# Mixture-of-experts tail of a graph and attention layer: expert rows scattered to token order inside the loop and reloaded densely

## What is computed

```
logits = xt @ router_w.T + router_b;  probs = softmax(logits)
topk_p, topk_i = top_k(probs, 2)
gates = sum(one_hot(topk_i) * topk_p)
for each expert e:
    h = gelu(xt @ w1[e].T + b1[e])
    acc += (h @ w2[e].T + b2[e]) * gates[:, e]
x = x + acc
```

## Time and profile before

| | us |
|---|---|
| median of 3 runs (lowest to highest) | 781.33 (780.14 to 784.73) |
| the profiled execution, its own time | 778.04 |
| its span, first to last record | 776.3 |
| PE busy | 699.3 (90%) |
| DVE busy | 456.4 (59%) |
| ACT busy | 232.4 (30%) |
| POOL busy | 132.5 (17%) |

### The profile page before, as it was taken

One profiled execution on the slowest core, in us unless ns is written; L12 is line 12 of the kernel. 1 busy time (PEld: TensorE's weight loads), 2 busy tenths in 40 slices (PEclk: granted clock), 3 DMA queues, 4 the chain that ended last, 5 costly groups with the idle time before them and its releaser, 6 DMA issues.

```text
span 776.3 us, 12270 instructions
## 1 busy us (share of the span) xinstructions
PE 699.3 (90%) x3759; PEld 450.8 (58%) x3760; DVE 456.4 (59%) x1388; ACT 232.4 (30%) x472; POOL 132.5 (17%) x191
## 2 busy tenths in 40 slices
PE   4888899999999999999999999999995499999934
PEld 2544455455555555555555788989783366676610
DVE  5538754278778787787854984353555233323336
ACT  2312211223233233232333333333342143344300
POOL 6055431000000000000000900020211110000064
PEclk9999999999999999999999999999996599999955
DMA  9600000073452707172555900010238695333467
GB/s 293 186 0 1 1 0 2 0 273 121 166 190 97 287 2 271 54 286 86 203 204 174 391 2 0 1 56 28 82 121 340 236 370 187 133 122 110 133 193 231
DMA packets 48883, 109.30 MB, mean 141 GB/s; under 512 B 6842, under 2 KB 6858, under 8 KB 46384
## 3 DMA queue, kind: packets, MB, share of 16 engines
q1 hardware_dynamic: 43616, 85.82, 30.7%
q0 software_dynamic: 4912, 20.60, 7.8%
q10 hardware_dynamic: 288, 2.10, 0.7%
HBM read 47.35 MB, written 61.16 MB: 140 GB/s over the span
## 4 chain that ended last, share of the span: by engine, by line
PE 79%; issue 5%; DVE 5%; POOL 4%; DMA 3%; ACT 2%; SPq 1%; POOLq 0%; DVEq 0%; ACTq 0%
PE bank L1284 12%; PE bank L1267 10%; PE bank L1435 7%; PE bank L1166 7%; PE bank L1235 7%; PE bank L1203 7%; PE bank L1448 6%; PE bank L1379 6%; PE bank L1322 6%; PE bank L1246 4%; PE bank L1307 4%; POOL arena L624 2%; PE bank L1406 2%; DMA arena<-in_wqkv 2%; DVE arena L887 1%
## 5 line engine op out<-in xcount | busy, mean ns | idle before, releaser
L887 DVE TENSOR_SCALAR arena<-iota,arena 125x128 f16<-125x128 f16 x392 | 113.2, 289 | 43.3 <-PE bank L1166 31.9
L889 DVE TENSOR_SCALAR arena<-iota,arena 125x320 f16<-125x320 f16 x392 | 120.3, 307 | 0.0
L698 ACT ACTIVATE arena<-bank 128x416 f32<-128x416 f32 (+1 forms) x120 | 62.3, 519 | 154.8 <-PE bank L1267 151.8
L1284 PE MATMUL bank<-arena 128*64 128x416 f32 (+1 forms) x480 | 97.2, 525 | 0.9 <-DVE arena L928 0.9
L928 DVE TENSOR_SCALAR arena<-bank 128x416 f32<-128x416 f32 (+1 forms) x120 | 68.1, 589 | 49.2 <-PE bank L1267 49.0
L1166 PE MATMUL bank<-arena 125*128 125x320 f16 x392 | 72.0, 302 | 8.7 <-DVE arena L889 8.5
L1235 PE MATMUL bank<-arena 128*128 128x416 f32 (+1 forms) x192 | 74.5, 537 | 2.7 <-DMA arena<-in_wqkv 1.4
L1435 PEld LDWEIGHTS bank<-arena 128*128 128x128 f32 x448 | 53.0, 198 | 20.7 <-issue 20.7
L1106 DVE COPY arena<-arena 128x1024 f32 x30 | 20.8, 694 | 74.5 <-issue 63.7
L1435 PE MATMUL bank<-arena 128*128 128x128 f32 x448 | 55.3, 283 | 9.9 <-issue 9.9
L1166 PEld LDWEIGHTS bank<-arena 125*128 125x128 f16 x392 | 32.4, 98 | 46.6 <-DVE arena L889 20.3
(11 more groups left out here) (228 smaller groups left out, 1171.4 us busy)
## 6 DMA issues: line engine op xcount, KB each, us to landing
slots<-arena SPq DMA_DIRECT2D x6, 5376.0 KB, 17.1
slots<-arena SPq DMA_DIRECT2D x2, 5120.0 KB, 16.5
arena<-in_ew POOLq DMA_DIRECT2D x9, 1024.0 KB, 7.0
arena<-slots SPq DMA_DIRECT2D x32, 256.0 KB, 2.8
slots<-arena SPq DMA_DIRECT2D x28, 256.0 KB, 2.0
arena<-in_ew SPq DMA_DIRECT2D x5, 1024.0 KB, 10.7
arena<-in_x SPq DMA_DIRECT2D x8, 512.0 KB, 6.9
arena<-in_gw SPq DMA_DIRECT2D x2, 2048.0 KB, 17.5
```

The costliest lines, as they stand in the source:

```text
L698: act.activation(probs[0:kt, s % NPB, 0, 0:n], bank[2 * (s % 2)][0:kt, 0:n], ACT.Relu).then_inc(p0_ready, 1)
L887: dve.tensor_scalar(ring[:, at_slot:at_slot + P], iota16[0:CE, 0:P], window_cols[:, i % WBUF, 1, k:k + 1], None, ALU.is_equal)
L889: dve.tensor_scalar(ring[:, at_slot + P:at_slot + OHW], iota16[0:CE, :], window_cols[:, i % WBUF, 0, k:k + 1], None, ALU.is_equal).then_in ...
L1284: ins = pe.matmul(bank[AV][DH * a:DH * a + DH, 0:n], v_sb[0:kt, t, h * DH:h * DH + DH], probs[0:kt, s % NPB, a, 0:n], start=(t == 0), stop ...
```

## The change

It does five things.

1. **A second DRAM tensor in token order.** `expert_rows` (`ys`) holds row k * 1250 + token for choice k, and behind these 2500 rows a spare row for each slot. A table `notes` in DRAM says for each slot to which row of `ys` its output goes. POOL first fills it with the spare rows (one DMA), and after each group's scatters of x rows it writes the real row numbers with indirect DMAs of 4-byte elements (20 in all, two per tile), at the places `note_at` that DVE computes from `slot` in `weigh` (three more small DVE operations for each group). At the end POOL reads the table into SBUF as `all_notes`.
2. **The store of the expert loop is a scatter.** POOL runs the loop too: it copies two columns of `all_notes` to `note_now`, waits for `y_saved`, scatters `y_sb` to `ys` with an indirect DMA of 128 rows, waits until both have landed and frees the two `y_sb` buffers (`y_free`), for which DVE now waits in place of `y_stored`.
3. **Dense reloads.** When the loop is over POOL raises `ys_done`; SP loads the rows of choice 0 and ACT those of choice 1, each with six DMAs, two tiles (512 KB) at a time, with one semaphore for each pair of tiles. No gather is left.
4. **Other queues.** The x rows of the loop are loaded by ACT, directly behind its copy of the turned rows. SP leaves the loop; it issues the nine late experts' weights and counts `w_ready`, the first three experts before it loads the first x rows.
5. **The end on PE and DVE.** The bias products rotate through four banks instead of two. DVE adds the first four tiles' bias before it waits for any reloaded row, and the bias of tile t + 4 after tile t.

The core of the diff:

```diff
@@ SP
+            for e in range(3):
+                count_expert(e)
             sp.wait_ge(route_ready, 1)
...
-            with sp.Fori(0, n) as j:
-                for a in range(2):
-
-                    sp.wait_ge(xgt_ps[a], j + 2)
-                    sp.dma_start(xg[:, a, :], rows_of(2 * j + 4 + a)).then_inc(xg_in[a], 16)
-                for a in range(2):
-                    sp.wait_ge(y_saved[a], j + 2)
-                    sp.dma_start(rows_of(2 * j + a), y_sb[:, a, :]).then_inc(y_stored[a], 16)
...
+            sp.wait_ge(xg_in[1], 16)
+            late = [3, 4, 5, 6, 7, 8, 12, 13, 14]
+            expert(late.pop(0))
+            expert(late.pop(0))
+            for e in range(3, EXP):
+                count_expert(e)
+                if late:
+                    expert(late.pop(0))
+
+            load_ys(sp, 0)
@@ POOL
+            for f, tiles in enumerate(FC_TILES):
+                pool.wait_ge(slots_ready, f + 1)
...
+                pool.wait_ge(gates_ready, f + 1)
+                for t in tiles:
+                    for k in range(2):
+                        pool.indirect_dma_start(
+                            out=notes, out_offset=bass.IndirectOffsetOnAxis(ap=note_at[0:rows(t), k, t:t + 1], axis=0),
+                            in_=note[0:rows(t), k, t:t + 1], in_offset=None).then_inc(noted, 16)
...
+            with pool.Fori(0, n) as j:
+                for a in range(2):
+                    i = pool.value_load(tile_at[0:1, bass.ds(2 * j + a, 1)], min_val=0, max_val=XS_TILES - 1)
+                    pool.tensor_copy(note_now[:, a:a + 1], all_notes[:, bass.ds(i, 1)]).then_inc(note_ready, 1)
+                for a in range(2):
+                    pool.wait_ge(note_ready, 2 * j + 2)
+                    pool.sem_inc(rows_landed, 1)
+                    pool.wait_ge(y_saved[a], j + 2)
+                    pool.sem_inc(rows_landed, 1)
                     pool.indirect_dma_start(
...
+                        out=ys, out_offset=bass.IndirectOffsetOnAxis(ap=note_now[:, a:a + 1], axis=0),
+                        in_=y_sb[:, a, :], in_offset=None).then_inc(y_stored[a], 16)
+                for a in range(2):
+                    pool.wait_ge(y_stored[a], 16 * j + 16)
+                    pool.sem_inc(y_free[a], 1)
+            pool.sem_inc(ys_done, 1)
@@ ACT, in the loop, behind the copy of the turned rows
+                    lies = act.value_load(tbase[0:1, bass.ds(2 * j + 4 + a, 1)], min_val=0, max_val=XS_ROWS - P)
+                    act.dma_start(xg[:, a, :], xs[bass.ds(lies, P), :]).then_inc(xg_in[a], 16)
...
+            load_ys(act, 1)
@@ DVE, the end
+            for t in range(4):
+                add_bias(t)
             for t in range(NT):
                 r = rows(t)
-                dve.wait_ge(gb_ps, t + 1)
-                link(dve.tensor_tensor(xr[0:r, t, :], xr[0:r, t, :], bank[2 + t % 2][0:r, :], ALU.add))
-                dve.sem_inc(gb_added, 1)
-                dve.wait_ge(yg_in[t], 32)
+                dve.wait_ge(yg_in[t // 2], 64 if t // 2 == LN_GROUPS - 1 else 32)
+                dve.wait_ge(gb_added, t + 1)
...
+                if t + 4 < NT:
+                    add_bias(t + 4)
```

More of the change, by code:

```diff
@@ L617, in _ @@
[L617 to L627 removed]
+            notes_v = notes.rearrange("(p t) c -> p (t c)", p=P)
```

98 lines of the change are left out of this document (58 added, 40 removed).

## The result

Measured in alternation on one chip: 781.13 us before, 785.58 us after (medians of 20 runs each; 779.07 to 784.93 and 781.01 to 794.30), ratio 1.0043 [1.0028, 1.0058]. The forecast of 774.1 us was wrong by 11.5 us and had the wrong sign. On chips 5, 10 and 14 the same kernel later took 774 to 776 us, as forecast; on chip 12 it took 782.7, again no faster than before. Which chip the first measurement ran on is not on record.

A forecast was written before the change was run, and what follows sets the result against it. PE alone was taken to bound the expert loop, POOL's gather pace the 38.8 us end. The end was to shrink by 7.2 us, loop and preparation costing 0: 781.33 - 7.2 = 774.1 us, range 771.0 to 779.0.

The forecast's parts named there:

- the preparation: Before the expert loop: note scatters, address work and table load were costed at 0, up to 3 us.
- Rival D: Notes, clearing and reordered queues delay x rows or loop start by 3 to 7 us; 777.5 to 781 us, chance 0.12.
- The last scatter: End: POOL starts 0.4 us after the last copy, landing takes 3.33, loop exit 0.3; 741.5, bounds 739.8 to 742.5.
- The first pair of tiles: End: first 1 MB of the two-queue reload usable after 6.1 us, bounds 4.8 and 7.2; DVE starts at 747.6.
- DVE: End: six tiles at 2.14 us and four at 1.46, 18.8 us in all; 19.6 with the old 2.28 kept.
- Rows in time: End: all 5 MB in by 758.7, last pair wanted at 763.4; slack 4.7 us, output stores costed at nothing.
- The table: Before the loop: note table loaded by about 620, register loads at 622, first output copy 625.04; slack 3 us.
- The handshake: Loop: POOL's added round takes 6.4 us, under 8.54, costing nothing; binds when a landing exceeds 5.4 us.
- rival A: Loop: handshake lags behind contended stores and PE stalls once or twice; 775 to 779 us, chance 0.16.
- SP's and ACT's parts: Loop: late experts' weights start about 2 us later, ACT gets some 1.9 us more work; both costed at nothing.
- rivals B, C and E: B: handshake binds throughout, 789.5 us, 0.06; C: reload starved, 776 to 777.4; E: gathers not holding DVE; C and E 0.13.

The follow-up runs named there:

- run with old banks: Kernel after with the old end on PE and DVE: two bias banks, each tile's bias added right ahead of its products; 782.11 us, one run.
- my first series: Chip 13: kernel before plus 20 unused note scatters, 4 bytes (782.68 us) or 512 bytes (782.76); kernel after with notes late (783.27), with 512-byte notes (775.38).

## Why the prediction failed, and where it held

**The step that failed** is the preparation, "I cost the preparation at 0, up to 3", with the reason that the earlier groups' notes "fall into POOL's long waits for DVE". They do: POOL has the time, and in the profiles without stalls their cost in the FC stage is nothing that can be read. But I priced the notes only by POOL's time and their landing. That beside them DVE, ACT and PE can stand still, I had no row for and no term. In the first measurement the FC stage became 7.0 us longer, on chip 12 8.8 and the routing another 2 (against the first profile of before; without stalls the FC stage varies by 3.3 us itself), against a gain of 8.8 at the end. Rival D had this effect by name (the gain eaten by 3 to 7 us, 777.5 to 781), with another mechanism, a chance of 0.12, and a price that was too small.

**What stays open.** Why some loadings stall and others don't was not found. The first measurement's chip, which is not on record, and chip 12 did, chips 5, 10 and 14 didn't (twice each on 5 and 10). So chip and loading can't be parted. That the notes cause the stalls is argued from their place alone: the first two stalls of both profiles begin while a group's notes are out, and end 9.3 to 9.6 us after its first one (the third, on chip 12, 6.3). Against it stands that landing events are missing from the first scatters of x rows on, before any note. A rival that no run tests is therefore a state of the loading that every scatter of POOL meets, so that the notes would add to it and not begin it. The kernel before, with the same 20 scatters of x rows, had neither stalls nor missing events in its profile; but that was another loading, and no profile of before was taken on chip 12. No stalling chip was given another kernel of mine, so whether 512-byte notes, or fewer of them, would be free of it wasn't tried. Since event records are missing in these stretches, a part of the recording of events in it can't be excluded either. And the sum doesn't close for the first measurement. By its stretches (-8.5 at the end by the medians of the table, +7 in the FC stage, +0.5 in the loop) the kernel after should have tied with before, as it did on chip 12. Its median was 4.5 us above that of before, and the profiled execution, 783.85, was one of the faster of the 20.

**Without the stalls the sum held.** Forecast 774.1; measured 774.7, 774.6, 773.9, 773.9 and 776.2. Point by point, by the first profile of after:

- *The last scatter*: reaction of POOL 0.8 us for the 0.4 taken, landing 2.70 for 3.33; the reload is issued 3.8 us after the last copy, forecast 4.0. Two errors that nearly cancel. (The upper bound of 742.5 is 0.3 too high by its own terms: 737.5 + 1.1 + 3.33 + 0.3 = 742.2.)
- *The first pair of tiles*: 5.3 us for 6.1, between the bounds of 4.8 and 7.2. By the rule of the Trainium skill, "DMA: Bandwidth & Descriptors", section "Issuing engines are not separate DMA queues", a second queue saves the time of issuing and no more. The trace agrees. The 5 MB of this reload, from two queues, had all landed 17.1 us after the first issue (755.94 to 773.0), as the 5 MB of the earlier trace rows from one queue. And the 0.8 us that the first pair gained is time of issuing: in the earlier trace rows SP issued the third of the three loads 0.81 us after the first, 5.25 us before POOL used them, while here SP and ACT issued the halves together. I had read the rule as "no gain at all", and so took 0.8 us too much. The third load of before:

```profile
420.87 0.43 SPq L412 DMA_DIRECT2D arena<-xn_rows  x1
```

- *DVE*: 2.05 and 1.45 us a tile for 2.14 and 1.46; 18.2 us for 18.8. The run with old banks gave 22.1, so the bias was worth 3.9, and the prediction's own rows (22.8 less 18.8) had said 4.0.
- *Rows in time*: right, no wait after the first pair. The end took 30.0 us for the forecast 31.6, a gain of 8.8 for 7.2.
- *The table*: in the first profile of after POOL read it at 626.27, 9 us ahead of DVE's first copy at 635.7, and nothing waited. With all notes sent late it did bind, and cost 8 us of loop.
- *The handshake*: 0 expected, up to 2.5; about 0.5 found by the medians of five and seven loops, in the way of rival A. Two to eight rounds run at 8.7 to 10.3 us, since one scatter of 8 us beside the weights puts POOL behind by more than a round gives back. What the working missed is how long the lag lasts once it is there. That it binds from a landing of 5.4 us on, no run tests.
- *SP's and ACT's parts, rivals B, C and E*: nothing of them was seen.

No version of mine beat the kernel after where it doesn't stall, and none was tried where it does.

## What to carry to other kernels

Split a time into stretches between points common to both kernels before explaining it; here the totals of one comparison hid a gain of 8.8 us at the end and a loss elsewhere, and one profile of the kernel before was quick by 2.4 us in a stretch where the change then seemed to lose. When a result contradicts a sum whose every term shows in the trace, run the unchanged kernel again on other chips before trying variants: my first series tested a cause on a chip where the effect may never have arisen. And when small scatters are added, look not only at their landing but at whether other engines start late beside them: compare the time from the producer's end to the consumer's start, instruction by instruction, and not the consumer's whole idle time.

## What the runs showed of the hardware

- Beside the note scatters, on two of seven loadings, ACT started up to 5.01 us and DVE up to 3.71 us after the end of what they needed from PE, where 0.04 is usual, and PE's operations came 0.7 us apart ahead of it. The lengths of the two largest delays were the same on both to 0.01 us. Landing events of POOL's scatters are missing in both profiles, the first of them some 5 us before the first note.
- A register load on PE's queue, 0.30 us as a rule, took up to 1.02 in the first profile of after and up to 1.31 in others of that loop, in rounds in which POOL's scatters were late; with the old stores by SP it took at most 0.33 in five profiles.
- The stretch up to the first score matmul took 153.2 to 154.6 us in the six profiles with a granted clock of 0.97 in 50 to 100 us, and 156.0 to 159.1 in the fourteen with 0.89 to 0.92.
- A 1 MB first pair of a reload, half of it from each of two queues, was in use 5.3 us after its issue, and all 5 MB were in 17.1 us after it, as long as 5 MB from one queue took.
